# Two transformer layers in one kernel: the Mamba pair loop keeps y and the convolution's tanh in PSUM, carries the states on GpSimd, and projects out in one float32 product

## The reference

```python
x = x + attention(xn) + xn @ binarized_w.T + bias
xn = layernorm(x)
x = x + mamba(xn) + gated_network(xn)

# mamba, 64 heads of 64 channels, state size 128
gate, hbc, dt = split(xn @ in_proj_w)
hbc = silu(causal_conv(hbc, 4 taps) + conv_b)
dt = softplus(dt + dt_bias);  A = -exp(A_log)
# in each chunk: inside part, plus what the state carried in adds
y = (C B^T * decay * dt) x  +  C * exp(cum) @ carried_state  +  D_param * x
state[c] = decay[c] * state[c - 1] + B^T (decay_to_end * dt * x)
hidden = y * silu(gate)
out = (hidden * rsqrt(mean(hidden^2) + EPS) * norm_w) @ out_proj_w
```

## Time and profile before

| what | value |
|---|---|
| median of 3 runs | 2196.16 us (2193.58 to 2197.35) |
| the profiled execution's own time | 2188.87 us |
| its span, first to last instruction | 2187.1 us |
| PE busy | 1935.1 us, 88% |
| DVE busy | 1669.4 us, 76% |
| ACT busy | 1358.3 us, 62% |
| POOL busy | 797.7 us, 36% |
| pairs of the four sequences | from about 275 to 560, 809 to 1090, 1348 to 1645 and 1886 to 2180 us |

### The profile page before, as it was taken

The page is one execution under the profiler, slowest core; times in us unless marked ns, Lnnn a source line. Parts: engine busy times, 40 slices in busy tenths (PEclk is TensorE's granted clock), DMA queues, the critical chain, the costliest instruction groups (busy, mean ns, idle before and its releaser), DMA issues.

```text
span 2187.1 us, 43967 instructions
## 1 busy us (share of the span) xinstructions
PE 1935.1 (88%) x13196; PEld 1581.5 (72%) x13196; DVE 1669.4 (76%) x3080; ACT 1358.3 (62%) x3106; POOL 797.7 (36%) x616
## 2 busy tenths in 40 slices
PE   5999988888899998888899998888889999888887
PEld 4888567777788856666678875766668887566676
DVE  4774589999677369999867736999987773599997
ACT  3662389999455147777745524777774542587775
POOL 2110167777300015555510002555550000255555
PEclk9999999999999999999999999999999999999999
DMA  5330255555322024444422102444442220244442
GB/s 186 121 117 1 84 179 187 193 195 185 100 81 77 30 66 137 145 145 144 139 81 80 58 30 80 134 144 144 144 130 82 86 68 12 84 148 146 145 139 88
DMA packets 119122, 247.88 MB, mean 113 GB/s; under 512 B 10448, under 2 KB 32144, under 8 KB 118928
## 3 DMA queue, kind: packets, MB, share of 16 engines
q1 hardware_dynamic: 119056, 247.04, 34.8%
HBM read 206.63 MB, written 40.37 MB: 113 GB/s over the span
## 4 chain that ended last, share of the span: by engine, by line
PE 37%; issue 26%; DVE 18%; ACT 12%; POOL 2%; DVEq 2%; ACTq 1%; DMA 0%; POOLq 0%
PE bank L648 18%; DVE conv_acc L1320 12%; ACT conv_acc L1075 4%; PE bank L861 4%; DVE state L1469 3%; ACT conv_th L1080 3%; PE bank L776 2%; PE both L648 2%; PE bank L768 2%; PE bank L748 2%; PE both L768 2%; ACT span_b L1157 2%; ACT place L1157 1%; ACT shared L1163 1%; DVEq L1320 1%
## 5 line engine op out<-in xcount | busy, mean ns | idle before, releaser
L648 PE MATMUL bank<-xn_r,w_r 128*128 128x512 f32 x2304 | 598.6, 410 | 12.3 <-POOL w_r L542 6.2
L648 PEld LDWEIGHTS bank<-xn_r,w_r 128*128 128x128 f32 x2304 | 432.1, 194 | 126.2 <-issue 33.6
L1320 DVE SCALAR_TENSOR_TENSOR conv_acc<-bank,conv_sb,conv_acc 128x511 f32<-128x511 f32 (+2 forms) x408 | 304.4, 746 | 73.7 <-ACT conv_acc L1075 40.0
L1005 ACT ACTIVATE place_r<-bank 128x512 fp32r<-128x512 f32 (+1 forms) x384 | 199.1, 563 | 194.3 <-PE bank L648 168.4
L1252 DVE TENSOR_TENSOR place_r<-bank,place_r 128x512 fp32r<-128x512 f32 (+1 forms) x384 | 231.1, 641 | 97.2 <-ACT place_r L1005 96.1
L536 POOL TENSOR_TENSOR rstd<-var_eps,minus_half 128x4 f32<-128x4 f32 (+2 forms) x12 | 9.7, 808 | 663.8 <-DVE var_eps L1265 663.8
L557 POOL TENSOR_TENSOR shared<-shared,c_t 128x768 f32<-128x768 f32 x128 | 236.4, 1847 | 0.0
L563 POOL TENSOR_TENSOR place_r<-place,place_r 128x512 fp32r<-128x512 f32 x128 | 177.4, 1386 | 143.9 <-ACT place_r L1058 143.9
L550 POOL TENSOR_TENSOR shared<-place,dec 128x384 f32<-128x384 f32 x128 | 107.6, 841 | 301.5 <-DVE place L1480 259.8
L648 PE MATMUL bank<-wo_r,place_r 128*128 128x256 f32 x1536 | 213.5, 288 | 2.4 <-POOL place_r L563 2.0
L844 PE MATMUL bank<-ident,place 128*128 128x128 f32 x512 | 84.4, 288 | 146.7 <-DVE place L1329 145.3
(11 more groups left out here) (155 smaller groups left out, 3624.6 us busy)
## 6 DMA issues: line engine op xcount, KB each, us to landing
place_r<-cum_rows SPq DMA_DIRECT2D x128, 512.0 KB, 4.6
w_r<-pair_split SPq DMA_DIRECT2D x96, 512.0 KB, 4.3
w_r<-qkv_split SPq DMA_DIRECT2D x48, 512.0 KB, 4.0
wo_r<-out_split SPq DMA_DIRECT2D x96, 256.0 KB, 2.6
pair_split<-w_r SPq DMA_DIRECT2D x32, 512.0 KB, 3.9
qkv_split<-w_r SPq DMA_DIRECT2D x16, 768.0 KB, 3.8
w_r<-qkv_split SPq DMA_DIRECT2D x48, 256.0 KB, 3.1
raw<-in_w_pair SPq DMA_DIRECT2D x32, 256.0 KB, 3.8
```

The source lines that it names most:

```text
L648: ins = mm(out, lhsT=w(a), rhs=m(b), start=(start and i == 0), stop=(stop and i == 2), **kw)
L1005: A(dst, src, ACT.Copy).then_inc(done, 1)
L1320: stt(out=conv_acc[:, back:W], in0=src[:, 0:W - back], scalar=conv_sb[:, ch, TAPS - 1 - back:TAPS - back], in1=conv_acc[:, back:W], op0=AL ...
```

## The change

Four edits, and what follows from them:

- y stays in PSUM bank 5: `base` writes it back there, and `gated` reads it there. `in_block` of n, which overwrites the bank, now waits for hidden of n-1 and not for y of n-1.
- The convolution's tanh is written over the bank that held its input, and `conv_end` reads it there.
- The states are carried on POOL, at the end of its step for the pair: ACT copies all three out of PSUM (128x384), and POOL does two rounds of a product into a small tile `carry` and a sum. Each of the four instructions waits for the one before.
- The output projection is one float32 product for each of four tiles, of pair n-1, at the end of PE's step (it was three float32r products, of pair n-2, ahead of `in_block`). `hid_high`, `hid_low` and `out_low` go, `out_high` writes plain float32 weights, and their transfers are half as long.
- ACT's order: the convolution's first tap is now ahead of `growth`, and `squares` ahead of the copy of the states.

```diff
+            def carry_states(b, n):
+                N = b * NPAIR + n
+                pool.wait_ge(s_state_ev, N + 2)
+                for c in range(1, NT - 1):
+                    if c > 1:
+                        pool.wait_ge(s_carried, N * 4 + c * 2 - 2)
+                    pool.tensor_tensor(carry[:].rearrange("p (h q) -> p h q", h=2),
+                                       state[:, c - 1, :].rearrange("p (h q) -> p h q", h=2),
+                                       dec[:, NT - 2 + c, bass.ds(n * 2, 2)].unsqueeze(2).to_broadcast([P, 2, HD]),
+                                       ALU.mult).then_inc(s_carried, 1)
+                    pool.wait_ge(s_carried, N * 4 + c * 2 - 1)
+                    pool.tensor_tensor(state[:, c, :], state[:, c, :], carry[:], ALU.add).then_inc(s_carried, 1)
...
                     weigh_c(b, n, par)
                     if not begin:
-                        hid_low(b, n - 1, 1 - par)
                         add_squares(b, n - 1)
+                    carry_states(b, n)
...
             def off_block(b, n, par):
-                pe.wait_ge(s_carried, N * 2 + 4)
+                pe.wait_ge(s_carried, (N + 1) * 4)
...
             def in_block(b, n, par):
-                pe.wait_ge(s_base_done, N + 1)
+                pe.wait_ge(s_hid_ready, N + 1)
...
             def project_out(b, n, par, begin, last):
-                pe.wait_ge(s_hid_split, N + 2)
+                pe.wait_ge(s_hid_ready, N + 2)
...
-                    ins = mm3(out_tile((6, 7), t), lambda i: hid_r[:, par, i, t * P:(t + 1) * P], lambda i: wo_r[:, par, i, :],
-                              begin and t % 2 == 0, last, skip_group_check=True)
+                    ins = mm(out_tile((6, 7), t), lhsT=hid[:, t * P:(t + 1) * P], rhs=wo_n[:, par, :],
+                             start=begin and t % 2 == 0, stop=last, skip_group_check=True)
...
                     make_states(b, n, par)
-                    if before > 1:
-                        project_out(b, n - 2, par, isinstance(n, int) and n == 2, False)
                     in_block(b, n, par)
+                    if before > 0:
+                        project_out(b, n - 1, 1 - par, isinstance(n, int) and n == 1, False)
...
-            def conv_tanh(k):
+            def conv_tanh(k, over):
                 act.wait_ge(s_taps_done, k + 1)
-                A(conv_th[:], conv_acc[:], ACT.Tanh).then_inc(s_conv_tanh, 1)
+                A(over[:], conv_acc[:], ACT.Tanh).then_inc(s_conv_tanh, 1)
...
                         spans(n + 1, 1 - par)
+                        pair_conv_start(b, n + 1)
                         if not begin:
                             act.wait_ge(s_off_done, N + 1)
                         growth(n + 1, 1 - par)
-                        pair_conv_start(b, n + 1)
...
-                    if not begin:
-                        hid_high(b, n - 1, 1 - par)
                     if more:
                         gate_tanh(b, n + 1, 1 - par)
...
+                    if not begin:
+                        squares(b, n - 1)
                     act.wait_ge(s_state_done, N + 2)
                     act.wait_ge(s_off_done, N + 1)
-                    copy_out(state[:, 0, :], bank[2][:, 0:P], s_state_ev)
-                    if not begin:
-                        squares(b, n - 1)
+                    copy_out(state[:].rearrange("p c q -> p (c q)"), bank[2][:, 0:W - P], s_state_ev)
...
-                        stt(out=y, in0=xs[:, par, :], scalar=d_sb[:, n:n + 1] if isinstance(n, int) else d_sb[:, bass.ds(n, 1)],
+                        stt(out=bank[5][:], in0=xs[:, par, :], scalar=d_sb[:, n:n + 1] if isinstance(n, int) else d_sb[:, bass.ds(n, 1)],
                             in1=bank[5][:], op0=ALU.mult, op1=ALU.add).then_inc(s_base_done, 1)
...
-                        tt(hid, y, gate[:, par, :], ALU.mult).then_inc(s_hid_ready, 1)
+                        tt(hid, bank[5][:], gate[:, par, :], ALU.mult).then_inc(s_hid_ready, 1)
...
-                    carry_states(n)
-                    if not begin and first(b):
-                        out_low(n - 1, 1 - par)
```

More of the change, by code:

```diff
@@ L134, in two_layers @@
         x_dt = place[:, 4 * W:6 * W].rearrange("p (a t q) -> p a t q", a=2, t=NT)
-        hid, y, square = (place[:, i * W:(i + 1) * W] for i in (6, 9, 10))
+        hid, square = place[:, 6 * W:7 * W], place[:, 10 * W:11 * W]
         span_b = sb("span_b", [P, 2 * W])
@@ L144, in two_layers @@
         spread = place_r[:, 4 * W:8 * W].bitcast(F32).rearrange("p (a w) -> p a w", a=2)
-        hid_r = place_r[:, 8 * W:12 * W].rearrange("p (a i w) -> p a i w", a=2, i=2)
         conv_acc = sb("conv_acc", [P, W])
-        conv_th = sb("conv_th", [P, W])
+        carry = sb("carry", [P, P])
         gate_th = sb("gate_th", [P, W])
@@ L622, in sequence @@
                 pair(NPAIR - 1, 1, False, more=False)
-                hid_low(b, NPAIR - 1, 1)
                 add_squares(b, NPAIR - 1)
@@ L1050, in out_high @@
                     act.wait_ge(out_saved[par], (n - par) * 8)
-                A(wo_r[:, par, 0, :], raw_out[:, par, :], ACT.Copy, scale=norm_sb[:, bass.ds(n, 1)]).then_inc(s_out_hi, 1)
-            def hid_high(b, n, par):
-                N = b * NPAIR + n
-                act.wait_ge(s_hid_ready, N + 2)
-                act.wait_ge(s_projected, N + 1)
-                A(hid_r[:, par, 0, :], hid, ACT.Copy).then_inc(s_hid_hi, 1)
+                A(wo_n[:, par, :], raw_out[:, par, :], ACT.Copy, scale=norm_sb[:, bass.ds(n, 1)]).then_inc(s_out_ready, 1)
             def squares(b, n):
@@ L1220, in sequence @@
                     v_high(b + 1, 0, 0, 0)
-                hid_high(b, NPAIR - 1, 1)
                 squares(b, NPAIR - 1)
@@ L1325, in conv_taps, with conv_end @@
                     conv_tap(k, ch, src, back)
-            def conv_end(k, dst):
+            def conv_end(k, dst, over):
                 dve.wait_ge(s_conv_tanh, k + 1)
-                stt(out=dst, in0=conv_th[:], scalar=1.0, in1=conv_acc[:], op0=ALU.add, op1=ALU.mult).then_inc(s_conv_silu, 1)
+                stt(out=dst, in0=over[:], scalar=1.0, in1=conv_acc[:], op0=ALU.add, op1=ALU.mult).then_inc(s_conv_silu, 1)
             def ffn_hid(b, f):
@@ L1429, in sequence @@
                     ln_out(b * 2 + 2, 7)
-                def out_low(n, par):
-                    dve.wait_ge(s_out_hi, n + 1)
-                    stt(out=wo_r[:, par, 1, :], in0=raw_out[:, par, :], scalar=norm_sb[:, bass.ds(n, 1)],
-                        in1=wo_r[:, par, 0, :].bitcast(F32), op0=ALU.mult, op1=ALU.subtract).then_inc(s_out_ready, 1)
                 def tail(n, par):
@@ L1458, in mixed @@
                               cb[:].rearrange("p t i -> p (t i)").unsqueeze(1).to_broadcast([P, 2, W]), ALU.mult)
-                def carry_states(n):
-                    N = b * NPAIR + n
-                    dve.wait_ge(s_state_ev, N + 2)
-                    for c in range(1, NT - 1):
-                        if c > 1:
-                            dve.wait_ge(s_carried, N * 2 + c + 1)
-                        for h in range(2):
-                            half = slice(h * HD, (h + 1) * HD)
-                            ins = stt(out=state[:, c, half], in0=state[:, c - 1, half],
-                                      scalar=dec[:, NT - 2 + c, bass.ds(n * 2 + h, 1)],
-                                      in1=bank[2][:, c * P + h * HD:c * P + (h + 1) * HD], op0=ALU.mult, op1=ALU.add)
-                        ins.then_inc(s_carried, 1)
                 def pair(n, par, more, begin=False):
@@ L1508, in sequence @@
                 pair(NPAIR - 1, 1, False)
-                if first(b):
-                    out_low(NPAIR - 1, 1)
                 if not last:
                     v_low(b + 1, 0, 0, 0)
-                dve.wait_ge(s_hid_ready, (b + 1) * NPAIR)
                 for step in tail(NPAIR - 1, 1):
```

46 lines of the change are left out of this document (19 added, 27 removed).

## The result

The changed kernel takes **2265.52 us** (median of 4 runs, 2262.42 to 2268.82), the kernel before 2196.14 us beside it: ratio 1.0318, interval 1.0300 to 1.0336. It is slower by 69 us. The forecast was 2308 us, range 2213 to 2357, so the direction and the range hold, and the size was too large. The profiled execution took 2268.82 us (span 2266.6), 80 us more than that of before, where I had reckoned 112.

The account below looks back on a forecast made before the run. DVE's loop bounds the kernel before; after the change POOL's queue ending in the carry does. -9 + 79 + 35 + 7 = +112 us on 2188.9 gives 2301, plus 7.3 to the median: 2308 us, range 2213 to 2357.

Parts of the forecast that it names:

- later sequences: Pairs of the later three sequences: 9.0 us a period against 9.10, off_block waiting for POOL's carry; -9 us.
- first sequence, POOL's chain: First sequence's pairs: split_low, weigh_c, add_squares, then the carry on POOL make 11.56 us for 8.84; +79 us.
- clock, first sequence: PE idle about 3 us before off_block brings half clock, 1.2 us a period in the first sequence; +35 us (0 to +48).
- ends of the sequences: Pair 30 of three sequences +10, after the last pair -5, last carry of the last sequence +2; together +7 us.
- The loop over POOL: Walk from off_block through projections, tap, growth, tanh, squares, add_squares and POOL's carry to the next off_block: 9.0 us, later sequences.
- S: Price of POOL's four carry instructions: two products, two sums, three hand-overs; 2.1 us, bounds 1.4 and 2.4.
- Tanh into PSUM "at nothing": Convolution's tanh written into PSUM and its end read from there: same lengths as before, 0.1 either way.
- 8.4 us for the latency loop: Later sequences' pair once DVE is no longer late: 9.10 less off_block's wait 0.27 and 0.45 for the taps.
- The clock stays up: Rival: no half clock although PE idles 3 us; +77, 2273 us; chance 0.2.
- The carry hides: Rival: S at 1.2, full clock; later sequences at 8.4 (-61), first at 10.66 (+53); about 2192 us; chance 0.08.
- 8.4 everywhere: Rival: the change's aim comes true, 8.4 us in all sequences, 2123 us; needs carries ahead of add_squares; chance 0.03.
- The low clock spreads: Rival: S at 2.3 or more, half of the later 87 periods lose 1.65 to the clock; 2390 us; chance 0.07.

Follow-up runs that it names:

- e6: The changed kernel with two extra unused 128x128 products on POOL, each followed by a wait for itself, ahead of the carry: 2443.49 us.
- e4: The changed kernel with 36 unused bf16 products of 128 columns on PE ahead of off_block, first sequence only: 2238.92 us.
- e1: The changed kernel with POOL's carry ahead of add_squares and ACT's copy of the states ahead of squares: 2160.71 us.
- e5: The changed kernel with ACT's w_high ahead of growth in the first sequence: 2233.21 us.
- e9: The changed kernel with the carry back on DVE and the convolution's tanh alone in SBUF again, y staying in PSUM: 2169.71 us.
- e2: The changed kernel with carry ahead of add_squares, states' copy ahead of squares, and POOL's split_low and xn_low behind the carry too: 2094.44 us.
- e3: The changed kernel with the carry alone put back on DVE at the end of its step, all else as changed: 2134.96 us.
- e7: The kernel before with only y and the convolution's tanh kept in PSUM (in_block waiting for hidden): 2166.95 us.

## Why the prediction was right in kind and too large in size

| term of the sum | forecast | measured | how |
|---|---|---|---|
| later sequences | -9 | -24 | 8.86, 8.85, 8.79 less 9.10, 9.10, 9.11, x 29 each |
| first sequence, POOL's chain | +79 | +69 | (11.23 - 8.85) x 29 |
| clock, first sequence | +35 | +23 | (12.01 - 11.23) x 29 |
| ends of the sequences | +7 | +4 | rest of the pairs' stages, which sum to +72 |
| between the pairs' stages | 0 | +7 | table of stages |
| sum | +112 | +79 | |

- **The loop over POOL: right.** Each step of the walk is in the rows above within about 0.1 us: to the tap 2.78 (forecast 2.79), growth 0.68 (0.69), tanh 0.73 (0.74), squares 0.48 (0.48), add_squares 0.88 (0.80), its own time 1.23 (1.28), the carry up to off_block 2.11 (2.22).
- **S (the four carry instructions and the waits between them): right as a sum, by two slips that cancel, which is luck.** The products take 0.40 (0.37 forecast), the sums 0.46 (0.42), the three hand-overs 0.09, 0.17 and 0.08 (0.17 each). From the first carry to the end of the last it is 2.06 (2.1), and off_block comes 0.05 later (0.12).
- **The term mis-sized in the later sequences** is a small difference of large numbers: 8.79 to 8.86 for 9.0. Above all S and its end were 0.11 shorter, and POOL's rows overlap by 0.05 (add_squares is 1.28 long, the next starts after 1.23). Over 87 periods this is 15 of the 33 us that I was off by.
- **First sequence: the same two slips.** split_low 1.24, weigh_c 1.78 and add_squares 1.23 from start to start, for 1.29, 1.85 and 1.28 (0.17 together), S and its end 2.10 for 2.22: 11.23 for 11.56.
- **The clock: right in place and sign, too large.** I had taken 1.2 us a period from the idle piece alone. The wait was there in each period, 2.4 to 2.9 us, but the low clock (1.2 of 2.4 GHz) came in some and not in others: the two pairs above have nearly the same wait before them (2.82 and 2.90) and clocks of 0.86 and 1.00. Of the 28 periods between the first and the last two, 18 have time at the low clock, and such a period loses 0.6 (11.85) to 1.95 (13.18), more at the upper end than the 1.65 that I had taken as the most. The rule of the Trainium skill (TensorE: Matmul & The Clock Gate, HAM oscillation — how this bites in real kernels), which would have given the loss in each period and +48, is further off; e6, where the wait is 3.6 to 4.1 us and no period of the first sequence is below 13.06, comes nearer to it. Counted in the same way, the periods of the first sequence with time at the low clock are none of 28 with waits of 0.8 to 0.9 us (e4), 7 at 1.6 to 1.7 (e1, five of them longer by it), 13 at 1.7 to 2.2 (e5), 18 at 2.4 to 2.9 (the change) and all 28 in e6. What decides from pair to pair stays open.
- **Tanh into PSUM "at nothing": wrong reason, right for the sum.** Its own length is nothing (0.60 for 0.63). But in the new order the end of the convolution would have met weigh_c in the first sequence. With the carry on DVE that is in the loop (e9, 9.54 for 8.66); in the change itself, where POOL's chain stands above it, it wasn't tried.
- **8.4 us for the latency loop: right,** but only without the carry on DVE: e1 and e2 show 8.35 in the later sequences, e3 with DVE's carry 8.72 or more. There the carry on DVE costs 0.37 a pair, where I had read 0.27 from off_block's wait.
- **Out projection:** 1.99 for 1.78 (0.22 a pass in attention's output, 0.25 here); it lies in PE's idle time, and e3, which has it, and e7, which has not, take the same in the second and third sequence (8.72 and 8.73).
- **Ends:** in pair 30 of the second sequence the period is 13.07 for 10.38, +2.7 where 3.4 were forecast; the other ends I did not part. The +7 between the pairs' stages was in no term; the clock reads 0.98 to 0.99 there for 0.99 to 1.00 before, and the cause is open.
- **From the profiled execution to the median:** I had added 7.3 us, by which the median of before lay above its profiled execution. For the changed kernel the median lies 3.3 below it, which makes 10.6 of the 42.5 us between 2308 and 2265.5; that is spread between runs, and no mechanism.
- **The rivals.** "The clock stays up" gave 2273, nearest to the 2265.5, but not by its mechanism: 23 us of clock loss are in the result, and e4 takes them out. "The carry hides" needed S at 1.3 or less, and S is 2.06. "8.4 everywhere" needed the carry ahead of add_squares, as I wrote; e2 built that, with the splits behind the carry too, and found 2094. "The low clock spreads" did not come in the change, but e6 shows it: with 1.1 us more in the chain, the later sequences get periods at the low clock as well.

## What to carry to other kernels

Before a short piece of work on a loop's critical path is moved to an idle engine, write down that engine's queue for the step and count everything that stands ahead of it: with a busy share of 37%, POOL was 131 us slower than DVE with the carry at the end of its step, and 40 faster with it directly behind weigh_c. Put what the next step waits for first and the bookkeeping (sums of squares, splits for later pairs) behind it. And look for products of two SBUF operands on VectorE that run beside GpSimd: one operand of each in PSUM was worth 28 us in the kernel before, 63 in the change with the carry on DVE, and 150 once the queue was right.

## What the hardware did that was not expected

A VectorE product of two SBUF operands (128x512) doesn't run slower beside GpSimd; by its times it waits for GpSimd's instruction to end. In four meetings it ends 0.54 to 0.56 us after it, whatever its own start: gated at 1608.74 behind weigh_c's 1608.19, and in the rows above 418.30 behind 417.76, 1602.90 behind 1602.34, 1607.70 behind 1607.14. In all 89 meetings of the kernel before in which weigh_c starts first, gated ends 0.54 to 0.56 after it and takes 1.34 to 1.93; undisturbed it takes 0.69. The shorter `out_low` (128x256) ends 0.28 after add_squares (e7). With y in PSUM 92 of the changed kernel's gated run beside weigh_c, and all take 0.69. It works the other way too: add_squares, started while the end of the convolution was still running, takes 1.71 for 1.28 in e9. The Trainium skill (SBUF — State Buffer, SBUF: two separate sides) states this as an exclusive lock that is held for the whole instruction, and these rows agree.

PSUM operands cost next to nothing here: tanh takes 0.60 into PSUM and 0.63 into SBUF, gated 0.69 with or without, and `base` 0.75 into PSUM and 0.74 into SBUF.

More work on PE made the kernel faster (e4, 27 us), since the granted clock stayed at 1.00 in the pairs where PE would have waited 2.8 us.
